# One batch of the front moved ahead of the first factorisation, and dense products set between small ones in a 64x64 solve

## The reference, cut to what matters

```python
def step(S, qkv):                      # one chunk of 128 tokens, one head
    Qc, Kc, Vc = qkv
    G = Kc.T @ Kc + RIDGE_EPS * I      # 64 x 64
    W = jnp.linalg.solve(G, Kc.T @ Vc)
    U = U0                             # 64 x 8
    for _ in range(POWER_K):           # 2
        U, _ = jnp.linalg.qr(W @ U)
    Wr = U @ (U.T @ W)
    S_new = DECAY_ALPHA * S + Wr
    return (S_new, SCALE * (Qc @ S_new))
```

## Time and profile before

| | |
|---|---|
| median of 3 runs | 1335.05 us (1333.93 to 1336.13) |
| the profiled execution, own time | 1337.31 us |
| its span in the trace | 1335.5 us |
| PE busy | 989.9 us, 17632 matmuls and as many weight loads |
| DVE busy | 1118.0 us |
| ACT busy | 661.8 us |
| POOL busy | 174.6 us |

### The profile page before, as it was taken

The page is one execution under the profiler, slowest core; times in us unless marked ns, Lnnn a source line. Parts: engine busy times, 40 slices in busy tenths (PEclk is TensorE's granted clock), DMA queues, the critical chain, the costliest instruction groups (busy, mean ns, idle before and its releaser), DMA issues.

```text
span 1335.5 us, 41205 instructions
## 1 busy us (share of the span) xinstructions
PE 989.9 (74%) x17632; PEld 762.0 (57%) x17632; DVE 1118.0 (84%) x3452; ACT 661.8 (50%) x1392; POOL 174.6 (13%) x118
## 2 busy tenths in 40 slices
PE   1693017596687899897899897782499838998597
PEld 0463016555576667776767777672477625765254
DVE  6875996699999599999599999689889699764996
ACT  3683017555344567645467645352246515655254
POOL 2420123201011001011001111001200020001000
PEclk9897558798688899899799899796699958999799
DMA  4321003300000001110002110013112100111001
GB/s 149 104 99 38 0 0 129 127 25 17 3 4 3 3 18 33 35 51 3 4 10 73 34 36 3 4 31 129 33 36 71 51 30 18 48 48 32 8 17 32
DMA packets 42693, 53.04 MB, mean 40 GB/s; under 512 B 2992, under 2 KB 25600, under 8 KB 42512
## 3 DMA queue, kind: packets, MB, share of 16 engines
q1 hardware_dynamic: 42512, 50.42, 11.4%
HBM read 32.53 MB, written 17.87 MB: 38 GB/s over the span
## 4 chain that ended last, share of the span: by engine, by line
PE 54%; DVE 31%; ACT 9%; issue 4%; POOL 1%; DMA 0%; DVEq 0%; ACTq 0%; POOLq 0%
PE a_bank L547 7%; PE a_bank L618 6%; PE a_bank L707 5%; DVE a_outer L1564 4%; DVE a_total L1570 4%; DVE a_outer L1568 4%; DVE a_blocks L1573 4%; PE a_bank L713 3%; PE a_bank L697 3%; PE a_bank L561 3%; PE a_bank L832 3%; PE a_bank L817 3%; PE a_bank L799 3%; PE a_bank L643 2%; PE a_bank L769 2%
## 5 line engine op out<-in xcount | busy, mean ns | idle before, releaser
L987 ACT ACTIVATE a_work<-a_bank 128x512 f32<-128x512 f32 (+1 forms) x193 | 109.3, 606 | 180.9 <-PE a_bank L675 138.5
L1487 POOL TENSOR_TENSOR a_root<-a_recip,a_half 128x32 f32<-128x32 f32 (+2 forms) x24 | 89.8, 3742 | 592.7 <-DVEq L1559 575.2
L675 PE MATMUL a_bank<-a_ident,a_blocks 128*128 128x128 f32 x256 | 38.5, 318 | 134.6 <-DVE a_blocks L1584 134.6
L1564 DVE TENSOR_TENSOR a_outer<-a_blocks,a_weight 128x62 f32<-128x62 f32 (+15 forms) x248 | 129.6, 523 | 0.0
L1570 DVE TENSOR_REDUCE a_total<-a_outer 128x62 f32<-128x62 f32 (+30 forms) x248 | 127.2, 513 | 0.3
L987 ACT ACTIVATE a_solve<-a_bank 128x512 f32<-128x512 f32 (+2 forms) x184 | 88.0, 526 | 69.2 <-PE a_bank L713 52.9
L1568 DVE TENSOR_TENSOR a_outer<-a_blocks 128x60 f32<-128x60 f32 (+14 forms) x240 | 119.4, 497 | 0.0
L1573 DVE TENSOR_TENSOR a_blocks<-a_blocks,a_outer 128x60 f32<-128x60 f32 (+14 forms) x240 | 118.6, 494 | 0.0
L675 PEld LDWEIGHTS a_bank<-a_ident,a_blocks 128*128 128x128 f32 x256 | 37.1, 203 | 135.5 <-DVE a_blocks L1584 135.5
L618 PE MATMUL a_bank<-a_scaled,a_blocks 128*128 128x352 f32 x256 | 92.6, 505 | 13.1 <-ACT a_blocks L987 13.1
L987 ACT ACTIVATE a_scaled<-a_bank 128x512 f32<-128x512 f32 (+2 forms) x133 | 66.8, 528 | 57.9 <-PE a_bank L697 46.2
(11 more groups left out here) (198 smaller groups left out, 2232.0 us busy)
## 6 DMA issues: line engine op xcount, KB each, us to landing
a_pair<-in_L_attn_x SPq DMA_DIRECT2D x16, 256.0 KB, 3.0
s_base<-a_pair SPq DMA_DIRECT2D x16, 256.0 KB, 2.8
s_xnt<-a_xb SPq DMA_DIRECT2D x12, 256.0 KB, 2.0
s_c<-a_xc SPq DMA_DIRECT2D x12, 256.0 KB, 2.6
a_cg<-s_c SPq DMA_DIRECT2D x12, 256.0 KB, 2.8
a_cc<-s_c SPq DMA_DIRECT2D x12, 256.0 KB, 3.4
a_blocks<-s_base SPq DMA_DIRECT2D x12, 256.0 KB, 3.4
s_x<-a_xc SPq DMA_DIRECT2D x12, 256.0 KB, 2.0
```

The source lines that it names most:

```text
L987: nc.scalar.activation(out, view, ACT.Copy, scale=scale).then_inc(emptied, 1)
L1487: nc.gpsimd.tensor_tensor(root[:, :, a:b], recip[:, :, a:b], half[:, :, a:b], ALU.pow).then_inc(roots_ok, 1)
L1564: known = ch.inc(V.tensor_tensor(terms, m[:, :, i:HB, 0:i], bcast(weight[:, :, 0:i], 2, n_i), ALU.mult))
```

## The change

Two edits.

**Front batch 8 ahead.** On DVE step 8 of the front is run before `lead(0)`, on POOL its two reciprocal roots before `roots(1)`, and on ACT its two normalisations before the empties of `lead_return(0)`. PE's and ACT's part of step 8 with banks stays where it was.

**The solve.** `scale_rows` and `squares` of `Tensor` become one generator `solved`, used by `schur` and `assemble`. The four dense known products of round k now stand inside scale of round k+1: one after each quarter of it (16 of the 64 small products). Round 3 has no scale after it, so its four stay together. Each takes its bank by a wait of its own. The yield between scale k+1 and the squares of round k is gone, on ACT as well, so that these six banks are one step for `woven`.

```diff
+            def solved(self, stationary, moving, half, mask, known):
+                parts = NQ // 32
+                def known_into(k, c):
+                    bank = self.u.fill(apart=True)
+                    at = 32 * k + 8 * c
+                    nc.tensor.matmul(bank[:].rearrange("p (q z c) -> p q z c", z=2, c=HB)[:, :, half], mask[:], known[:, at:at + 8, :],
+                                     start=True, stop=False, skip_group_check=True)
+                    return bank
+                def scale(k, before):
+                    two, four = self.u.fill(2, apart=True), []
+                    for i in range(8):
...
+                        if before is not None and i % 2 == 1 and i < 7:
+                            four.append(known_into(before, i // 2))
+                    last.then_inc(filled, 2)
+                    if before is not None:
+                        four.append(known_into(before, 3))
+                    return four
+                mark = self.u.n + 2
+                scale(0, None)
+                yield
+                for k in range(parts):
+                    ready = mark
+                    if k + 1 < parts:
+                        mark = self.u.n + 2
+                        four = scale(k + 1, k)
+                    else:
+                        four = [known_into(k, c) for c in range(4)]
+                    self.u.need(ready, apart=True)
...
+                    last.then_inc(filled, 4)
+                    yield
@@ Scalar.front, Scalar.solved @@
+            def ahead(self, b):
                 self.normalise(b + 2, 0)
                 self.normalise(b + 1, 1)
+            def front(self, b):
+                if b != 2 * GB_N:
+                    self.ahead(b)
...
                         self.scale_rows(k + 1)
-                        yield
                     self.squares(k, dst, scale)
                     yield
@@ run @@
+            e.ahead(2 * GB_N)
             straight(e.lead_return(0))
@@ gpsimd @@
-                for b in range(2 * GB_N):
+                for b in range(2 * GB_N + 1):
                     front(b)
                 roots(1)
-                for b in range(2 * GB_N, B):
+                for b in range(2 * GB_N + 1, B):
                     front(b)
@@ vector @@
+                front(2 * GB_N)
                 lead(0)
-                for b in range(2 * GB_N, B):
+                for b in range(2 * GB_N + 1, B):
                     front(b)
```

More of the change, by code:

```diff
@@ L498, in front_open @@
                 pass
+            def ahead(self, b):
+                pass
             def gates(self):
@@ L688, in lead_return @@
                 self.at["lead"] = self.u.mark()
[L690 to L700, removed]
@@ L708, in squares @@
                                      start=True, stop=False, skip_group_check=True)
[L709 to L714, removed]
@@ L715, in squares @@
-                last.then_inc(filled, 4)
+                    return bank
+                def scale(k, before):
+                    two, four = self.u.fill(2, apart=True), []
+                    for i in range(8):
+                        for c in range(4):
+                            for s in range(2):
+                                q = 32 * k + 8 * c + i
+                                last = nc.tensor.matmul(two[s][HB * c:HB * c + HB, i * DH:(i + 1) * DH], stationary(s, q), moving(s, q),
+                                                        start=True, stop=True)
+                        if before is not None and i % 2 == 1 and i < 7:
[4 more added lines that the diff above has]
+                    return four
@@ new lines, in solved @@
+                mark = self.u.n + 2
[9 more added lines that the diff above has]
+                    self.u.need(ready, apart=True)
+                    for i in range(8):
+                        for c in range(4):
+                            for s in range(2):
+                                both = scaled[HB * c:HB * c + HB, (2 * k + s) * 8 + i, :]
+                                last = nc.tensor.matmul(four[c][rows(s, None), i * DH:(i + 1) * DH], both, both, start=False, stop=True,
+                                                        skip_group_check=True)
+                    last.then_inc(filled, 4)
+                    yield
@@ L722, in schur @@
                 self.u.need(self.at["lead"], apart=True)
[L724 to L728, removed]
-                yield
[L730 to L736, removed]
+                m = yield from self.solved(lambda s, q: work[rows(s, 0), q, :], lambda s, q: beside(eyes[0][rows(s, 0)], gram[rows(s, 0), q, :]),
+                                           1, minus[1], gram)
                 yield from self.to_problems(gram, m)
@@ L745, in assemble @@
                 self.pe.sem_inc(schur_read, 1)
[L747 to L759, removed]
+                yield from self.solved(lambda s, q: work[rows(s, 1), q, :], lambda s, q: beside(kept[rows(s, 1), q, :], eyes[1][rows(s, 1)]),
+                                       0, minus[0], kept)
             def moments(self, src, mark):
@@ L1022, in gates, with ahead @@
                 self.move(gates_t[:], bank[:, 0:2 * B].rearrange("p (i b) -> p i b", b=B))
-            def front(self, b):
+            def ahead(self, b):
                 self.normalise(b + 2, 0)
                 self.normalise(b + 1, 1)
+            def front(self, b):
+                if b != 2 * GB_N:
+                    self.ahead(b)
                 if b >= 2 * GB_N:
```

4 lines of the change are left out of this document (removed).

## The result

The changed kernel took 1369.91 us (median of 4 executions, 1365.15 to 1371.25) beside 1335.59 us for the kernel before (1333.93 to 1339.07): ratio 1.0247, 95% interval 1.0215 to 1.0279, 34.3 us slower. The profiled execution took 1365.15 us, with a span of 1363.3 us.

A forecast was written before the change was run, and what follows sets the result against it. The end was taken to be set in turn by the front stretch before schur(0), DVE until 417, then schur(1..3) and assemble(1..3). Terms -2.0 - 6.6 + 6.3 + 0 = -2.3 us gave 1332.8 us, range 1321 to 1346.

The forecast's parts named there:

- Where it is decided: Front stretch before schur(0), DVE until 417, then schur(1..3) and assemble(1..3) set the end; assemble(0) can gain nothing.
- Front batch 8: Step 8 fits the gap before lead(0), cost 0; stretch up to schur(0) gains: -2.0 us, bounds -5.7 and +1.5.
- A solve by itself: schur(1..3), running alone: dense products fill instruction-transfer stalls, 28.7 us each, -2.2 each, -6.6 for three.
- A fifth: Share of a solve running alone taken to be at 1.2 GHz: 27.6 + 0.2 x 5.5 = 28.7 us.
- The joints at 1.2 GHz: Small-to-dense switches in a solve at 1.2 GHz: 2.3 us a solve, included in the 33.1 us bound.
- I take 0: Each dense product's bank waited for singly: cost 0, at most 1.9 us for twelve waits.
- A woven solve: assemble(1..3), beside write: new waits 2.1 and 0.7, joints 2.3, less 3.0 saved; +2.1 us each, +6.3.
- the 3.0 "saved": assemble(1..3): stalls and low clock saved by the new form, 3.0 us on average per solve.
- Rival 1: Woven solves decide: c0 and c2 of assemble(1..3), joints bare, 5.1 us each, 1341.8 us; chance 0.29.
- Sum: -2.0 - 6.6 + 6.3 + 0 for assemble(0) = -2.3 us, 1332.8 us.
- The forecast's own range: Half the bounds of each term: 1327 to 1338 us; the forecast's chance 0.34.
- Rival 4: The solve's edit fills nothing, joints bare everywhere: +20.2 us, 1355.3 us; chance 0.03.

The follow-up runs named there:

- fewer waits: Banks waited for four and two at a time: in the changed kernel 1348.34 us, 1.0133; with the new solve only in schur(1..3), 1337.61 us, 1.0073.
- lone only: Kernel before with dense products between the quarters of scale only in the solves that run alone, schur(1..3): 1338.50 us, ratio 1.0073.
- order alone: Kernel before without the solve loop's yields on TensorE and ScalarE, dense products still in one block behind scale: 1343.48 us, ratio 1.0115.
- front only: Kernel before with front batch 8 ahead and the old solves: 1330.39 us, ratio 1.0013.
- middle block: Kernel before, in schur(1..3) the four dense products of a round in one block after the fourth of scale's eight steps: 1333.09 us, ratio 1.0043.

## Why the prediction was wrong

It gave 1332.8 us (1321 to 1346); it is 34.3 us slower than before. By its own steps:

- **Where it is decided** was right: nothing was lost outside the solves, and `assemble(0)`, though of the new form, still ended ahead of `lead(1)`'s result (3.89 us at 414.64).
- **Front batch 8** ahead: cost 0 was right, with step 8 in the gap and `lead(0)` still at 116 in most executions. Of the -2.0, ratio 1.0013 shows nothing. `schur(0)` in the new form lost 3.4 us instead. The waits of the changed kernel are where I put them: PE waited 5.02 us before batch 11 and 1.24 before batch 10, and DVE 12.81 us, until 209.54, for h of batch 11. The wait was lengthened and nothing saved.
- **A solve by itself, -2.2 each: +4.0.** The mechanism of the filling was right: stalls are filled (32.8 to 20.5 us), and where the clock stays up the solve takes what was worked out, 27.6: 27.4 and 26.7 us with fewer waits, 27.7 in lone only. Three terms were mis-sized.
  - "A fifth" at 1.2 GHz: of 15 lone solves eight ran at 1.2 GHz for three quarters of the time or more (PEclk 0.57 to 0.62), and the mean over the 15 is 0.686, so 63% of the time. The forecast took it that dense products nearer together would keep the level up; no row of the kernel before showed that.
  - The joints at 1.2 GHz: there a round is 9.2 us, not 2.0 + 3.7 + 2.0 + 0.6: a joint costs more there, (9.2 - 7.7) / 3 = 0.5 us a pair, so the bound of 33.1 us should have been 35.3.
  - "I take 0" for the single waits: in the old form twelve of them cost 1.5 us, some 0.1 us each, inside the bounds given.

  With the measured share and joint my own formula gives 27.6 + 0.63 x 7.7 = 32.5 us, and with the waits 34.0, an estimate, beside 34.3 measured. The twelve instructions a solve, added up from solve to solve, also moved the first stall of the second lone solve into its first dense product and that of the third to six matmuls behind it. Without them the whole change costs 1.33% instead of 2.5 to 3.5%; whether by their number or by their place is not shown.
- **A woven solve, +2.1: +7.7.** The order alone is +4.3, its waits 2.1 and 0.7 as forecast (1.24 to 2.16 and 0.70 with the changed solve); missing was the clock, which fell behind eight of the nine waits of 2 us. Joints less the 3.0 "saved" by stalls and clock were put at -0.7 and came to 7.7 - 4.3 = +3.4: here nothing was saved on average: nine of the 15 solves ran at the low level behind c0 and took 5.5 us more than the other six. Rival 1 named the place and had its price, 5.1, a third too low.
- **Sum**: 3 x 4.0 + 3 x 7.7 + 3.4 = 38.5 us. The terms are means over five executions; the five medians lie 33.5 to 44.8 us above the kernel before, mean 38.3, the first of them 34.3.
- **The forecast's own range**: half the bounds of each term, added, make 1322 to 1346, not 1327 to 1338; the result lies outside either.
- **Rival 4** came nearest in its time (1355.3), by filling nothing. That isn't what happened: the stalls were filled. The fetches that the Trainium skill's page "Runtime: NRT & Kernel Launch", section Instruction fetch mechanics, has hidden by the pace of dispatch stand in every profile here (1.27 and 1.35 us above), so this case's traces disagree with that page.

Open: why the clock takes one course or the other at the same position. The first lone solve has the same instruction offset in both kernels with fewer waits, 33.4 us in one and 29.7 in the other; the changed kernel's own first lone solve, always stalled first behind its 152nd matmul, took 34.8, 32.8 and 31.2 us. Also whether the fewer waits help the woven solves at all (46.6, 46.5, 43.3 against a mean of 47.2 and a spread of 6.7), and whether a low clock in one stage carries over to the next. No version here beats the kernel before; front only and the middle block come within 0.1 and 0.4%.

## What to carry to other kernels

Filling a stall with work is worth it only while TensorE stays at its high level: price the filled form at both levels, with the joints too. A code edit that adds instructions to an engine near the pace of its instruction transfers moves every later stall; measure such a change at more than one offset, by medians and not by one profile each, before it is judged. Of a wait in a woven stage the price is its length and often the low level behind it: here 4.3 us a solve for 2.8 us of waits.

## What the runs showed of the hardware

- The stalls come at fixed places of TensorE's program: in all five profiles of the new form the lone solves first stalled behind their 152nd, 161st and 168th matmul. 36 more instructions ahead moved it in the second lone solve from the 179th to the 161st (27.7 and 35.9 us in one profile each, PEclk 0.94 and 0.57; the medians hardly differ).
- More work in about the same time: dense products issued twice between the quarters came with a granted clock of 0.90 to 0.95 and solves of 34.9 us, where the changed kernel had 0.57 to 0.89 and 34.3 us. In one block behind scale the same addition left it at 0.82 to 0.86 and was paid whole.
- A joint between 32x32 and dense matmuls costs 0.25 us a pair at 2.4 GHz and about 0.5 us at 1.2: a round of the new form is 4 x 1.01 + 1.52 = 5.6 us against 4.85, and 9.2 against 7.7, with three pairs more.
- The same solve can take either course of the clock: `assemble(1)` of the changed kernel took 43.4 us in two executions (PEclk 0.88) and 49.6 in a third (0.76).
